# A gated cross-attention layer in float32: the first loads in smaller pieces, the last output chunk in two halves

## What is computed

```python
q = (layernorm(x) @ wq)          # 32 heads of 128
k = (ctx @ wk); v = (ctx @ wv)   # 8 heads of 128 each, shared by 4 query heads
q, k = apply_rope(q), apply_rope(k)
attn = softmax(q @ k.T / sqrt(128) + mask)
x = x + tanh(g_xattn) * (attn @ v) @ wo

xf = layernorm(x)
routing = softmax(xf @ gate_w.T)               # 8 experts
in_scale, out_scale = routing @ in_channel_scale, routing @ out_channel_scale
x = x + tanh(g_ffn) * ((xf * in_scale) @ sign(weight).T * out_scale + bias)
```

## Time and profile before

| what | value |
|---|---|
| median of 3 runs | 1468.59 us (1467.74 to 1469.41) |
| the profiled execution, its own time | 1468.77 us |
| span of that execution in the trace | 1467.0 us |
| TensorE busy | 1446.3 us, 99% |
| VectorE busy | 998.9 us, 68% |
| GpSimd busy | 719.9 us, 49% |
| ScalarE busy | 570.1 us, 39% |

### The profile page before, as it was taken

One profiled execution on the slowest core, in us unless ns is written; L12 is line 12 of the kernel. 1 busy time (PEld: TensorE's weight loads), 2 busy tenths in 40 slices (PEclk: granted clock), 3 DMA queues, 4 the chain that ended last, 5 costly groups with the idle time before them and its releaser, 6 DMA issues.

```text
span 1467.0 us, 21329 instructions
## 1 busy us (share of the span) xinstructions
PE 1446.3 (99%) x6800; PEld 1197.1 (82%) x6800; DVE 998.9 (68%) x2141; ACT 570.1 (39%) x927; POOL 719.9 (49%) x594
## 2 busy tenths in 40 slices
PE   7999999999999999999999989999999999999998
PEld 6988888888888888888888867888888888877786
DVE  6858888888888888888888876636246247436653
ACT  6922222222222222222222258438348348225551
POOL 6935554554555545545555456426226226036554
PEclk9999999999999999999999999999999999999999
DMA  8822122212221222122212298888998989943321
GB/s 309 289 101 65 39 80 74 69 52 70 79 70 43 79 71 71 50 71 79 71 43 72 72 312 274 292 263 275 353 353 268 369 272 298 302 152 111 113 79 65
DMA packets 114898, 226.40 MB, mean 154 GB/s; under 512 B 12272, under 2 KB 23024, under 8 KB 114704
## 3 DMA queue, kind: packets, MB, share of 16 engines
q1 hardware_dynamic: 110224, 210.03, 44.7%
q10 hardware_dynamic: 4608, 15.53, 2.9%
HBM read 167.84 MB, written 57.67 MB: 154 GB/s over the span
## 4 chain that ended last, share of the span: by engine, by line
PE 89%; issue 3%; DVE 2%; POOL 2%; DMA 2%; SPq 1%; ACT 1%; POOLq 0%; ACTq 0%
PE bank L52 19%; PE bank L53 19%; PE bank L54 19%; PE bank L966 8%; PE bank L967 8%; PE bank L968 8%; PE bank L990 5%; POOL last_rows L1424 1%; PE bank L1005 1%; SPq L727 1%; DMA w_raw<-in_wo 1%; DVE stats L293 1%; DMA w_raw<-in_wkv 1%; DVE x_lo L324 1%; PE xt_ps L152 0%
## 5 line engine op out<-in xcount | busy, mean ns | idle before, releaser
L52 PE MATMUL bank<-x_hi,w_hi 128*128 128x512 f32 x1024 | 398.5, 389 | 0.3 <-issue 0.3
L54 PE MATMUL bank<-x_hi,w_lo 128*128 128x512 f32 x1024 | 398.3, 389 | 0.0
L53 PE MATMUL bank<-x_lo,w_hi 128*128 128x512 f32 x1024 | 398.3, 389 | 0.0
L1363 POOL TENSOR_TENSOR q_lo<-rot,q_hi 128x512 fp32r<-128x512 f32 x128 | 165.4, 1293 | 184.0 <-ACT q_hi L1126 183.1
L52 PEld LDWEIGHTS bank<-x_hi,w_hi 128*128 128x128 f32 x1024 | 192.2, 188 | 40.4 <-issue 0.5
L53 PEld LDWEIGHTS bank<-x_lo,w_hi 128*128 128x128 f32 x1024 | 192.2, 188 | 39.9
L54 PEld LDWEIGHTS bank<-x_hi,w_lo 128*128 128x128 f32 x1024 | 192.2, 188 | 39.8
L1126 ACT CAST q_hi<-rot 128x512 fp32r<-128x512 f32 x128 | 79.5, 621 | 346.2 <-DVE rot L1487 254.2
L1429 POOL TENSOR_TENSOR w_lo<-w_raw,w_hi 128x512 fp32r<-128x512 f32 x100 | 127.1, 1292 | 169.5 <-ACT w_hi L1178 169.5
L1559 DVE TENSOR_TENSOR project<-bank,project 64x512 fp32r<-64x512 f32 x128 | 87.5, 684 | 144.8 <-ACT project L1186 142.8
L1370 POOL TENSOR_TENSOR pt_lo<-pt,pt_hi 128x512 fp32r<-128x512 f32 x64 | 82.5, 1290 | 153.7 <-ACT pt_hi L1136 153.6
(11 more groups left out here) (143 smaller groups left out, 2656.4 us busy)
## 6 DMA issues: line engine op xcount, KB each, us to landing
project<-probs_scratch SPq DMA_DIRECT2D x160, 256.0 KB, 6.8
w_raw<-in_wo SPq DMA_DIRECT2D x100, 256.0 KB, 4.6
p_left<-probs_scratch SPq DMA_DIRECT2D x96, 256.0 KB, 5.7
w_raw<-in_wq SPq DMA_DIRECT2D x32, 512.0 KB, 5.2
probs_scratch<-pt_hi SPq DMA_DIRECT2D x64, 256.0 KB, 2.6
probs_scratch<-pt_lo SPq DMA_DIRECT2D x64, 256.0 KB, 3.2
last_rows<-in_x SPq DMA_DIRECT2D x8, 1024.0 KB, 8.4
x_scratch<-last_rows SPq DMA_DIRECT2D x8, 1024.0 KB, 9.1
```

The costliest lines, as they stand in the source:

```text
L52: pe.matmul(out, hi, rhs_hi, start=first, stop=False, **kw)
L53: pe.matmul(out, hi, rhs_lo, start=False, stop=False, **kw)
L54: return pe.matmul(out, lo, rhs_hi, start=False, stop=last, **kw)
L1363: nc.gpsimd.tensor_tensor(q_lo[:, c], rot[:, c], q_hi[:, c].bitcast(F32), ALU.subtract).then_inc(q_lo_ready, 1)
```

## The change

The context is loaded and split in three pieces: tiles 0 and 1, tiles 2 and 3, tiles 4 to 7 (`third(q)`). Unit 0 is loaded and split in two halves. On Sync's queue these alternate: context third 0, unit 0 half 0, context third 1, unit 0 half 1, context third 2, unit 1. No semaphore is added for this: half 0 of unit 0 counts on the one of unit 2, and context third 2 on the one of unit 3, so `arrivals(n)` expects one load more there. TensorE waits for the thirds of the context before tiles 0, 2 and 4 of unit 0.

In the last chunk of the last block VectorE multiplies the first 256 columns, which GpSimd adds; VectorE then multiplies the other 256 and adds them itself (`last_half`), into the same `y`. Sync's store of that chunk waits for both.

```diff
--- before.py
+++ after.py
@@ -143,6 +143,14 @@
         def half(h):
             return slice(h * KH, (h + 1) * KH)
 
+        def third(q):
+
+            return slice(2 * q, 2 * q + 2) if q < 2 else half(1)
+
+        def arrivals(n):
+
+            return 16 * (n // 4 + 1 + (n % 4 >= 2))
+
         def turn_tile(pe, i):
             if i == 0:
                 pe.wait_ge(ident_in, 16)
@@ -159,7 +167,7 @@
                 if n >= 4:
                     sp.wait_ge(w_lo_ready, 2 * (n - 3))
                 elif n >= 2:
-                    sp.wait_ge(ctx_lo_ready, 2)
+                    sp.wait_ge(ctx_lo_ready, 3)
                 sp.dma_start(raw(n), a["wkv"][n] if n < NU else a["wq"][0, n - NU]).then_inc(w_in[n % 4], 16)
 
             def store_keys(gp):
@@ -172,10 +180,13 @@
                 for c, part in enumerate((v_hi, v_lo)):
                     sp.dma_start(scratch["values"][c, g], part[:, g % 2].bitcast(F32)).then_inc(v_stored[g % 2], 16)
 
-            for h in range(2):
-                src = a["ctx_t"].rearrange("(k p) t -> p k t", p=P)[:, half(h)]
-                sp.dma_start(ctx_raw[:, half(h)], src).then_inc(ctx_in[h], 16)
-                load_unit(h)
+            ctx_src = a["ctx_t"].rearrange("(k p) t -> p k t", p=P)
+            sp.dma_start(ctx_raw[:, third(0)], ctx_src[:, third(0)]).then_inc(ctx_in[0], 16)
+            sp.dma_start(raw(0)[:, half(0)], a["wkv"][0][:, half(0)]).then_inc(w_in[2], 16)
+            sp.dma_start(ctx_raw[:, third(1)], ctx_src[:, third(1)]).then_inc(ctx_in[1], 16)
+            sp.dma_start(raw(0)[:, half(1)], a["wkv"][0][:, half(1)]).then_inc(w_in[0], 16)
+            sp.dma_start(ctx_raw[:, third(2)], ctx_src[:, third(2)]).then_inc(w_in[3], 16)
+            load_unit(1)
             for i in range(XB):
                 sp.dma_start(x_in[:, i], a["x"][i * P:(i + 1) * P, :]).then_inc(x_in_sem[i], 16)
             for n in range(2, UNITS):
@@ -197,12 +208,12 @@
                     elif n >= 4:
                         pe.wait_ge(k_read, (n - 4) // 2 + 1)
                     for h in range(2):
-                        if n == 0:
-                            pe.wait_ge(ctx_hi_ready, h + 1)
-                            pe.wait_ge(ctx_lo_ready, h + 1)
                         pe.wait_ge(w_hi_ready, 2 * n + h + 1)
                         pe.wait_ge(w_lo_ready, 2 * n + h + 1)
                         for k in range(h * KH, (h + 1) * KH):
+                            if n == 0 and k in (0, 2, 4):
+                                pe.wait_ge(ctx_hi_ready, k // 2 + 1)
+                                pe.wait_ge(ctx_lo_ready, k // 2 + 1)
                             last = three(pe, kv_ps[n % 4][:, 0:CTX], w_hi[:, n % 2, k, :], w_lo[:, n % 2, k, :],
                                          ctx_hi[:, k, :], ctx_lo[:, k, :], k == 0, k == KT - 1)
                         last.then_inc(kv_done, 1)
@@ -212,10 +223,16 @@
         @block.scalar
         def _(act):
             def split_unit(n):
-                act.wait_ge(w_in[n % 4], 16 * (n // 4 + 1))
+                act.wait_ge(w_in[n % 4], arrivals(n))
                 for h in range(2):
-                    wait(act, kv_done, 2 * (n - 2) + h + 1)
-                    nc.scalar.copy(w_hi[:, n % 2, half(h)], raw(n)[:, half(h)]).then_inc(w_hi_ready, 1)
+                    split_half(n, h)
+
+            def split_half(n, h):
+                wait(act, kv_done, 2 * (n - 2) + h + 1)
+                nc.scalar.copy(w_hi[:, n % 2, half(h)], raw(n)[:, half(h)]).then_inc(w_hi_ready, 1)
+
+            def context_high(q):
+                nc.scalar.copy(ctx_hi[:, third(q)], ctx_raw[:, third(q)]).then_inc(ctx_hi_ready, 1)
 
             def load_x(i):
                 act.wait_ge(xn_ready, i - XB + 1)
@@ -242,11 +259,16 @@
             act.dma_start(ident[:], a["ident"]).then_inc(ident_in, 16)
             act.dma_start(cos_k[:], a["cos_k"]).then_inc(tables_in, 16)
             act.dma_start(sin_k[:], a["sin_k"]).then_inc(tables_in, 16)
-            for h in range(2):
-                act.wait_ge(ctx_in[h], 16)
-                nc.scalar.copy(ctx_hi[:, half(h)], ctx_raw[:, half(h)]).then_inc(ctx_hi_ready, 1)
-                if h == 0:
-                    split_unit(0)
+            act.wait_ge(ctx_in[0], 16)
+            context_high(0)
+            act.wait_ge(w_in[2], 16)
+            split_half(0, 0)
+            act.wait_ge(ctx_in[1], 16)
+            context_high(1)
+            act.wait_ge(w_in[0], 16)
+            split_half(0, 1)
+            act.wait_ge(w_in[3], 16)
+            context_high(2)
             for n in range(NU + 2):
                 if n + 1 < UNITS:
                     split_unit(n + 1)
@@ -324,9 +346,9 @@
                     last = nc.vector.tensor_tensor(x_lo[at], xt_ps[2 * (i % 2) + j][:], x_hi[at].bitcast(F32), ALU.subtract)
                 last.then_inc(x_lo_ready, 1)
 
-            for h in range(2):
-                dve.wait_ge(ctx_hi_ready, h + 1)
-                nc.vector.tensor_tensor(ctx_lo[:, half(h)], ctx_raw[:, half(h)], ctx_hi[:, half(h)].bitcast(F32),
+            for q in range(3):
+                dve.wait_ge(ctx_hi_ready, q + 1)
+                nc.vector.tensor_tensor(ctx_lo[:, third(q)], ctx_raw[:, third(q)], ctx_hi[:, third(q)].bitcast(F32),
                                         ALU.subtract).then_inc(ctx_lo_ready, 1)
             statistics(0)
             dve.wait_ge(tables_in, 32)
@@ -683,6 +705,10 @@
 
             return pieces[m // 2][:, 2 * (m % 2):2 * (m % 2) + 2, :]
 
+        def ended(i, c):
+
+            return isinstance(i, int) and i == NB - 1 and c == NC - 1
+
         def x1_loads(i):
 
             return 16 * (i // 2 + 1)
@@ -870,6 +896,8 @@
                 if has(i, 1):
                     for c in range(NC):
                         sp.wait_ge(y_ready, NC * (i - 1) + c + 1)
+                        if ended(i - 1, c):
+                            sp.wait_ge(y_part_ready, NC * NB + 2)
                         dst = out.rearrange("(i n p) (h w) -> i n h p w", p=P, n=NT, h=2)[bass.ds(i - 1, 1), c // 2, c % 2]
                         sp.dma_start(dst.rearrange("o p w -> (o p) w"), y[:, c]).then_inc(y_stored[c], 16)
 
@@ -1421,7 +1449,8 @@
                 pool.wait_ge(y_part_ready, NC * i + c + 1)
                 pool.wait_ge(x1b_ready, i + 1)
                 wait(pool, y_stored[c], 16 * i)
-                nc.gpsimd.tensor_tensor(y[:, c], y_part[:, c % 2], x1b[j][t][:, h * HW:(h + 1) * HW], ALU.add).then_inc(y_ready, 1)
+                w = HW // 2 if ended(i, c) else HW
+                nc.gpsimd.tensor_tensor(y[:, c, 0:w], y_part[:, c % 2, 0:w], x1b[j][t][:, h * HW:h * HW + w], ALU.add).then_inc(y_ready, 1)
 
             def split_low(k, h):
                 i = k % WO_BUFS
@@ -1631,7 +1660,17 @@
                 dve.wait_ge(f_done, NC * i + c + 1)
                 dve.wait_ge(os_copied, NC * i + c + 1)
                 wait(dve, y_ready, NC * i + c - 1)
-                nc.vector.tensor_tensor(y_part[:, c % 2], f_ps[c % 2][:], out_scale[:, c % 2], ALU.mult).then_inc(y_part_ready, 1)
+                w = HW // 2 if ended(i, c) else HW
+                nc.vector.tensor_tensor(y_part[:, c % 2, 0:w], f_ps[c % 2][:, 0:w], out_scale[:, c % 2, 0:w], ALU.mult).then_inc(y_part_ready, 1)
+
+            def last_half(j):
+
+                i, c, at = NB - 1, NC - 1, slice(HW // 2, HW)
+                nc.vector.tensor_tensor(y_part[:, c % 2, at], f_ps[c % 2][:, at], out_scale[:, c % 2, at], ALU.mult).then_inc(y_part_ready, 1)
+                dve.wait_ge(y_part_ready, NC * NB + 1)
+                dve.wait_ge(x1b_ready, NB)
+                dve.wait_ge(y_stored[c], 16 * i)
+                nc.vector.tensor_tensor(y[:, c, at], y_part[:, c % 2, at], x1b[j][NT - 1][:, HW + HW // 2:], ALU.add).then_inc(y_part_ready, 1)
 
             def first_block(hp):
 
@@ -1771,6 +1810,7 @@
                     scaled(i - 1, 3)
 
             over_blocks(dve, slot)
+            last_half((NB - 1) % 2)
 
 
 _OUT = ((B, S, D), "float32")
```

2 lines of the change are left out of this document (1 added, 1 removed).

## The result

The change took **1472.95 us** in the median of 20 executions, the kernel before 1469.24 us in 20 beside it: ratio 1.002, 95% interval 1.0014 to 1.0026. It is slower by 3.7 us between the medians. The forecast of 1467.9 was wrong, and so was its range. Two executions of the change, at 1618 and 1815 us, were in a slow state with a granted clock of 0.85 and 0.75; the ratio leaves them out, and without them the median is 1472.77, 3.5 us over. The medians stand for distributions: 13 of the other 18 executions of the change lie above 1471.5 us and 3 of the 20 of the kernel before, while the lowest of either are 1468.43 and 1467.74.

What follows compares the result with a forecast made beforehand. TensorE was taken to set the pace alone only from 49.60 us, waiting on other engines before, with a serial row at the end. 1468.77 - 0.52 (tail) - 0.20 (head) = 1468.05, less 0.18 for the runs' median: 1467.9 us, range 1466.3 to 1469.3.

Steps and rivals of the forecast that it cites:

- Tail, -0.52: Last chunk: splitting multiply and add in halves ends the last add at 1463.95 in place of 1464.47.
- Head, start: First stage: first matmul at about 7.4, 1.8 us earlier; unit 2 and what leads to it gain 0.20 us.
- the lock on ctx_lo: VectorE's ctx_lo at 9.94 no longer stands behind GpSimd's w_lo: 0.25 us regained, ending at 11.16 instead of 11.41.
- The bytes ahead of each point of the stream stay the same: Load stream: half megabytes still complete by about 5.3, 7.06 and 8.87, unit 1 by 10.15.
- Rstd, xn, the load of x tile 3, w_hi and w_lo of unit 2 each follow 0.25 earlier: Chain from GpSimd's w_lo of unit 1 to unit 2: each step 0.25 us earlier, of which 0.20 was counted.
- 0 and -0.25: Bounds in us on the head's gain, given as -0.20, since how much the x load passes on was open.
- The one by the stream of loads: Rival: smaller transfers bring context third 2 at 10.26, the chain 1.14 us later, 1469.2 us in all; chance 0.12.
- a split of third 2 after 9.6: Sign of the load stream rival: ScalarE splits context third 2 after 9.6 us.
- The rival by the clock: Rival: TensorE's stop between unit 0's halves delays the clock's rise, at worst to 19; about 1468.5 us, no change; chance 0.08.
- The rival with TensorE as the bound: Rival: TensorE bounds from its first matmul on, so 1.84 us reach the end, 1466.2 us; chance 0.10.
- 0.92 on "no change": Chance that the time lies within 0.2% of 1468.59 us, between 1465.65 and 1471.5.

Runs made afterwards that it cites:

- the head alone: The change's new loads and splits with the last chunk as in the kernel before: 1470.21 us, ratio 1.0008 to the kernel before.
- the PSUM version: The whole change, with two sine products of the key rotation written to idle PSUM columns so its last two operations read one SBUF tensor each: 1470.11 us, ratio 1.0001.
- the late kernel before: The kernel before with two unused statistics operations on VectorE after x tile 3 lands, 1.2 us of delay: 1472.95 us, ratio 1.0022.
- the PSUM rotation and its loads: The kernel before, its loads kept, with the rotation's sine products in PSUM: 1469.14 us, ratio 0.9995; also with the last chunk in halves: 1468.55, 0.9994.
- pair with and without PSUM: The change repeated beside the change with the rotation's sine products in PSUM: 1473.72 us without, 1470.11 with.
- pair of late kernels: The kernel before with VectorE delayed 1.2 us at x tile 3, without and with the rotation's sine products in PSUM: 1472.95 and 1470.31 us.
- its three groups: The unaltered change timed beside the kernel before in three groups of runs: 1472.95, 1470.64 and 1473.72 us, ratios 1.002, 1.0013 and 1.002.

## Why the prediction was wrong

- **Tail, -0.52: right up to the last add.** 1.51 us in place of 2.03, operation by operation, in the change and alone. From that add to the end of the span, which the sum left as it was, the profiles take 0.25 more in the mean, so from the first multiply to the end 4.59 became 4.32, -0.27. Either size is too small to be measured in the time.
- **Head, start: right, as far as it went.** First matmul 7.35 (7.4), the lock on ctx_lo gone (1.23 us; forecast 1.22), the early matmuls worth nothing. In the profile of the head alone the queries come 0.31 earlier (0.20). A slip that decides nothing: the earlier trace rows have 20 matmuls in their 4.40 us and none is missing, and half 0 was done at 10.25, not 9.95.
- **"The bytes ahead of each point of the stream stay the same": the first step that failed.** Bytes stay, the pace doesn't. Third 2 was to be split at 8.87 and was at 9.34. "Rstd, xn, the load of x tile 3, w_hi and w_lo of unit 2 each follow 0.25 earlier" fell with it: ScalarE split unit 2 at 17.77 in place of 16.59, and tile 3's statistics, which were to begin at about 20.65, began at 22.84. The bounds "0 and -0.25" on what the x load passes on had no side above zero, though the row I rested on (4.68 us with the DMA share at 1.00) says that such a load depends on all the others in flight; it took 6.43.
- **The lock left out between the x load and unit 2: the step that cost most of the 3.7 us.** The sum has no term for it. I measured the lock in the earlier trace rows, used it on ctx_lo and on the tail, and didn't look for the other pairs that it could hit. The rotation reads two SBUF tensors at 23.94 and 24.28, GpSimd's next w_lo was to start at 24.70, just behind them. With tile 3 late they took 1.33 and 1.48 us in place of 0.42 each, and TensorE stood 3.27 us. A prediction that listed those pairs would have put a cliff behind a tile 3 that is later than GpSimd by 0.7 us.
- **The rivals.** The one by the stream of loads had the direction right and the threshold wrong: it counted from third 2's landing, deciding at 0.77, where 0.47 with a 2 us later tile 3 was enough; its own sign, a split of third 2 after 9.6, didn't show. It passed lateness on one for one (+0.6 in all). Without the lock that is what happens (1.62 at unit 2, 1.70 at the queries in the PSUM version); with it, in the late kernel before, 1.2 us became 3.25. The rival by the clock named a wrong place: the clock did fall, after the 3.27 us stop at 26.7 and not always, while behind the halves of unit 0 it was up at 15.07 (the rival had counted 15.6) and cost nothing. The rival with TensorE as the bound is refuted: 1.89 us earlier, and later in the end.
- **The chances.** With 0.92 on "no change" I took three executions that spread over 1.7 us as the spread of the kernel. Over 156 executions it is 1467.54 to 1474.09, and 21 of them are above 1471.5. That the kernel before lives near the cliff too is likely (with the PSUM rotation and its loads, 1 of 33 is above), but no profile of such an execution was taken.

Shown: the lock on the rotation, its price, and that it stands for most of the difference of the medians (pair with and without PSUM, pair of late kernels). Known from one pair of profiles only: the share of the clock. Open: why the six smaller transfers, and unit 2 and tile 3 behind them, land late and scattered; and why the same change was 3.7, 0.7 and 4.0 us behind in its three groups. While the change waits for tile 3 little moves:

```profile
20.00:21.00 1.00, 1.00 (x9) 1.00 (x10) 0.00 (x0) 0.54 (x2) 1.00 (x2) 1.00 0.19 78
```

A share of 0.19 is that of three of 16 engines, as if most had done their part. In that stretch Sync had nothing new to add: its next load waits for w_lo of unit 2 and left at 21.01, 19.85 before. Why the load of tile 3 itself goes on until 22.8 no run tells.

## What to carry to other kernels

When one lock or contention is found in a trace, list every pair of instructions that it could hit and the slack that keeps each apart; two engines released by the same event keep their distance, and here they met in each of the four profiles where that event came last. Bound what a reordered stream of loads does to the last load behind it from above as well, since what hangs on it may be a step and not a slope. Where a kernel's executions scatter by a few us, one profile shows a phase and not the kernel: count executions above a line as well as medians.
